# Cross-attention keys kept whole and rotated ahead, one norm's statistics used for two, all values made in the scan

## The reference

```python
xm = _ln(_ln(x, ln1_g, ln1_b), ln_g, ln_b)
xc = silu(conv3(xm @ w1_w + w1_b));  v = silu(xm @ v1_w + v1_b)
y  = _selective_ssm(xc, ...)                 # 128 channels x 16 states, scan over 256 steps
x1 = (y * v) @ w2_w + w2_b + x
a  = gelu(_ln(x1, ln2_g, ln2_b) @ ff1_w + ff1_b) @ ff2_w + ff2_b + x1
x  = _layernorm(x + a)                                          # "post0"
lat = _ln(x, ln_lat_g, ln_lat_b)                                # a norm of a norm
ctx = _ln(context, ln_ctx_g, ln_ctx_b)                          # 2 x 512 tokens
q = lat @ Wq;  k, v = split(ctx @ Wkv)                          # 16 heads of 64
k = apply_rope(k, cos, sin)
attn = softmax(clip(q k^T / 8, -11, 11))                        # per head, 256 x 512
x = _layernorm(x + (attn v) @ Wo + bo)                          # "post1"
```

## Time and profile before

| | us |
|---|---|
| three runs, median (lowest to highest) | 533.27 (531.43 to 534.46) |
| the profiled execution, whole | 532.46 |
| its span in the trace | 530.7 |
| TensorE busy | 439.2 (83%) |
| VectorE busy | 313.8 (59%) |
| ScalarE busy | 205.0 (39%) |
| POOL busy | 141.0 (27%) |

### The profile page before, as it was taken

The page is one execution under the profiler, slowest core; times in us unless marked ns, Lnnn a source line. Parts: engine busy times, 40 slices in busy tenths (PEclk is TensorE's granted clock), DMA queues, the critical chain, the costliest instruction groups (busy, mean ns, idle before and its releaser), DMA issues.

```text
span 530.7 us, 7338 instructions
## 1 busy us (share of the span) xinstructions
PE 439.2 (83%) x2780; PEld 265.4 (50%) x2788; DVE 313.8 (59%) x741; ACT 205.0 (39%) x257; POOL 141.0 (27%) x133
## 2 busy tenths in 40 slices
PE   0538978699999999889999888698567989978794
PEld 0206655354444445665777655345323544564384
DVE  4669954636766665542511487864696775236554
ACT  0555613143333233115333358774133444626500
POOL 3205643337767666400200400000100000003300
PEclk9867997989999999989999896999997999989898
DMA  8501000000004111060142230000000000010000
GB/s 305 214 25 44 2 1 0 1 2 1 0 1 158 41 41 40 19 228 1 60 64 31 49 61 0 3 3 1 0 3 0 2 2 3 1 31 0 0 1 20
DMA packets 7359, 19.37 MB, mean 37 GB/s; under 512 B 1750, under 2 KB 3126, under 8 KB 6806
## 3 DMA queue, kind: packets, MB, share of 16 engines
q1 hardware_dynamic: 7324, 18.91, 12.0%
HBM read 17.26 MB, written 1.15 MB: 35 GB/s over the span
## 4 chain that ended last, share of the span: by engine, by line
PE 40%; DVE 26%; POOL 15%; issue 13%; ACT 5%; DMA 1%; POOLq 0%; another core or an unknown queue 0%; DVEq 0%
PE ps L1190 38%; POOL big L540 7%; DVE ps L1043 4%; POOL big L547 4%; POOL rstd L490 2%; DVE ps L861 2%; DVE big L866 2%; DVE stats L773 2%; DVE mx_a L1047 2%; POOL big L522 2%; DVE normed L783 1%; ACT big L700 1%; PE ps L1202 1%; PE ps L1564 1%; DVE meanvar L776 1%
## 5 line engine op out<-in xcount | busy, mean ns | idle before, releaser
L1190 PE MATMUL ps<-big,late 128*32 128x256 f32 (+4 forms) x792 | 102.7, 386 | 12.4 <-DVE mx_x L1043 5.2
L1190 PE MATMUL ps<-late,big 128*128 128x128 f32 (+1 forms) x448 | 64.4, 276 | 3.6 <-DVE mx_x L1043 2.0
L1190 PEld LDWEIGHTS ps<-big,late 128*32 128x32 f32 (+3 forms) x800 | 39.5, 117 | 54.4 <-issue 23.1
L726 ACT ACTIVATE big<-ps 128x1024 f32<-128x1024 f32 x48 | 49.0, 1023 | 39.8 <-PE ps L1190 39.4
L488 POOL TENSOR_SCALAR vareps<-meanvar 128x4 f32<-128x4 f32 (+1 forms) x11 | 2.5, 229 | 221.1 <-DVE meanvar L776 221.1
L1190 PEld LDWEIGHTS ps<-late,big 128*128 128x128 f32 (+1 forms) x448 | 44.8, 152 | 27.4 <-issue 20.2
L664 ACT ACTIVATE big<-ps 128x1024 f32<-128x1024 f32 x32 | 32.8, 1024 | 64.8 <-PE ps L1190 47.0
L540 POOL TENSOR_TENSOR big<-big 128x512 f32<-128x512 f32 x32 | 40.5, 1267 | 43.2 <-DVE big L926 43.2
L1043 DVE CUSTOM_DVE_ANT_0 ps<-ps,big 128x512 f32<-128x512 f32 x64 | 42.5, 718 | 12.1 <-PE ps L1190 9.1
L1190 PE MATMUL ps<-big 64*128 64x256 f32 (+1 forms) x320 | 47.5, 410 | 1.7 <-POOL big L547 1.0
L926 DVE TENSOR_SCALAR big<-big 128x1024 f32<-128x1024 f32 x32 | 25.3, 790 | 39.7 <-ACT big L664 39.7
(11 more groups left out here) (231 smaller groups left out, 686.0 us busy)
## 6 DMA issues: line engine op xcount, KB each, us to landing
attn_w<-in_w_x SPq DMA_DIRECT2D x1, 2560.0 KB, 13.2
big<-parts_kx SPq DMA_DIRECT2D x18, 128.0 KB
late<-in_w_up SPq DMA_DIRECT2D x1, 2048.0 KB, 7.7
late<-in_w_dn SPq DMA_DIRECT2D x4, 512.0 KB, 4.0
attn_w<-in_w_up SPq DMA_DIRECT2D x1, 1024.0 KB, 6.4
attn_w<-in_w_dn SPq DMA_DIRECT2D x1, 1024.0 KB, 9.3
parts_kx<-ctx_r SPq DMA_DIRECT2D x1, 768.0 KB, 4.4
rowv<-in_rowv SPq DMA_DIRECT2D x1, 576.0 KB, 3.8
```

What stands on the lines that cost most here:

```text
L726: nc.scalar.activation(ex1[:, n % 3, :].rearrange("p (r n) -> p r n", r=2), ps[:, 2 * (n % 2):2 * (n % 2) + 2, :], ACT.Exp, scale=scale).t ...
L1190: return nc.tensor.matmul(o, lhsT, rhs, start=start, stop=stop, skip_group_check=shared)
```

## The change

1. **Room for all keys.** `kT0` becomes eight tiles, two where they were and six in the region `mid`, which is free after the scan. The buffers of the products move to `dtmp` and one piece of `big1`.
2. **Keys ahead.** Nine tiles (`K_FIRST`) are made ahead of the loop, in banks that a table names. In the loop one tile for each pair follows (9 to 15, pairs 0 to 6): the query at u = 0, key halves at u = 1 and 2, nothing at u = 3. All `idle_work` between the scan and the loop goes.
3. **Values.** All 16 groups are made in the scan, one a step from step 0.
4. **One norm for two.** The statistics of `summed` serve post0 and lat: with variance v the second norm of a normed row has the factor (v(1 + eps) + eps^2)^-0.5. POOL computes this root first and post0's behind it; VectorE writes `normed` (lat) first, then rotates tiles 6 to 8, then writes `x`.
5. **POOL's order.** After ln2's root and after the two roots, POOL waits until the normalised tiles are written, before it goes on with rotations and residual sums.
6. **ScalarE's tables.** A dummy activation with Gelu before ln2's transposes and with Exp after the Gelus loads the function tables there. The sign product of `rope0` moves ahead of the scan.

```diff
-NORMS = ("ln1", "ln", "ctx", "ln2", "post0", "lat", "post1", "post2", "post3", "post4", "post5")
+NORMS = ("ln1", "ln", "ctx", "ln2", "lat", "post0", "post1", "post2", "post3", "post4", "post5")
-        kT0 = big1(0, [P, 2, B * CS])
+        kT0 = [big1(1024 * c, [P, B * CS]) if c < 2 else mid(5120 - 1024 * (c - 2), [P, B * CS])
+               for c in range(NPAIR)]
+        kt1 = (dtmp[:, 0, :], dtmp[:, 2, :])
+        kt2 = (dtmp[:, 1, :], big1(3584, [P, CS]))
+        FF_BANKS = (0, 3, 5)
+        K_FIRST = 9
+        def key_banks(n):
+            return ((6, 7), (6, 7), (4, 3), (1, 2), (6, 7), (4, 3), (6, 7), (5, 2))[n] if n < 8 else (7, 6)
```

On POOL:

```diff
+            rotated0(0)
             root("ln2")
+            pool.wait_ge(norm_out, normed_tiles("ln2"))
+            for n in (1, 2, 3):
+                rotated0(n)
             pool.wait_ge(S["x2_done"], 1)
             link(nc.gpsimd.tensor_tensor(resid[:], x[:], rv4("ff2_b"), ALU.add))
             nc.gpsimd.tensor_tensor(resid[:], resid[:], x2[:], ALU.add).then_inc(S["res_ready"], 1)
-            for b in range(B):
-                rotated0(0, b)
-            root("post0")
-            root("lat")
-            rotated0(1, 0)
+            rotated0(4)
+            k = NORMS.index("lat")
+            pool.wait_ge(norm_var, k + 2)
+            link(nc.gpsimd.tensor_scalar(vareps[:, 0:NJ], meanvar[:, k, 0:NJ, 1], 1.0 + EPS, EPS * EPS,
+                                         ALU.mult, ALU.add))
+            nc.gpsimd.tensor_tensor(rstd[:, k, 0:NJ], vareps[:, 0:NJ], neghalf[:, 0:NJ],
+                                    ALU.pow).then_inc(norm_rstd, 1)
...
+            nc.gpsimd.tensor_tensor(rstd[:, k + 1, 0:NJ], vareps[:, 0:NJ], neghalf[:, 0:NJ],
+                                    ALU.pow).then_inc(norm_rstd, 1)
+            pool.wait_ge(norm_out, normed_tiles("lat"))
+            for n in range(5, K_FIRST):
+                rotated0(n)
             pool.wait_ge(norm_out, normed_tiles("post0"))
             nc.gpsimd.tensor_tensor(resid[:], x[:], rv4("bo0"), ALU.add).then_inc(S["res_ready"], 1)
...
-                if u in (0, 3) and 2 <= c + 1 < NPAIR or n == 3:
-                    rotated0(c + 1, u // 3)
+                if u == 2 and K_FIRST + c < B * NPAIR:
+                    rotated0(K_FIRST + c)
```

On ScalarE:

```diff
-                u = s - 3
-                if 0 <= u < V_EARLY:
-                    evac0(u // 2, f"v{u % 2}")
+                if s:
+                    evac0((s - 1) // 2, f"v{(s - 1) % 2}")
...
+            set_table(ACT.Gelu)
             to_cols(xT[:], 0, "xT_ps", "xT_done", v("ln2_g"), v("ln2_b"), 2)
...
+            set_table(ACT.Exp)
             to_cols(xT[:], 0, "xT_ps", "xT_done", v("lat_g"), v("lat_b"), 3)
```

On VectorE:

```diff
+            rotary(0)
             dve.wait_ge(S["y_ps"], NG // 4)
...
-            layernorm("ln2", x2[:], normed)
+            layernorm("ln2", x2[:], normed, lambda: rotary(1))
+            for n in (2, 3, 4):
+                rotary(n)
...
-            add_and_norm(4, "ff2_ps", 1, 2, "post0")
+            link(nc.vector.tensor_tensor(flat(summed), ps[:, 1, :], flat(resid), ALU.add))
...
+            rotary(5)
+            for i, dst in enumerate((normed, x)):
+                dve.wait_ge(norm_rstd, k + i + 1)
+                for j in range(NJ):
+                    nc.vector.tensor_scalar(dst[:, j, :], summed[:, j, :], meanvar[:, k, j, 0:1],
+                                            rstd[:, k + i, j:j + 1], ALU.subtract, ALU.mult
+                                            ).then_inc(norm_out, 1)
+                if i == 0:
+                    for n in range(6, K_FIRST):
+                        rotary(n)
-            layernorm("lat", x[:], normed, lambda: rotary(1, 0))
...
+                    if u == 2 and K_FIRST + c < B * NPAIR:
+                        rotary(K_FIRST + c)
```

On TensorE, in the scan and in the loop:

```diff
-                if 0 <= s - 2 < V_EARLY:
-                    values0((s - 2) // 2, s % 2)
+                values0(s // 2, s % 2)
...
-                if 2 <= c + 1 < NPAIR or c == 0 and u:
-                    project0(c + 1, u)
+                later = K_FIRST + c
+                if c + 1 < NPAIR and u == 0:
+                    pe.wait_ge(S["k0_mul"], 2 * later)
+                    mm(ps[:, 6, :], w_x0[:, c + 1, 3, :], xT[:]).then_inc(S["q0_ps"], 1)
+                elif c + 1 < NPAIR and u == 1:
+                    keys0(later, (0,))
+                elif c + 1 < NPAIR and u == 2:
+                    pe.wait_ge(S["q0_done"], c + 2)
+                    keys0(later, (1,))
```

139 lines of the change are left out of this document (68 added, 71 removed).

## The result

| device us | before | changed |
|---|---|---|
| median (four runs each, same chip) | 532.57 | 506.54 |
| lowest to highest | 531.43 to 534.46 | 506.17 to 507.45 |
| ratio, 95% interval | 1 | 0.951 (0.948 to 0.954) |
| profiled execution: time, span | 532.46, 530.7 | 506.76, 505.0 |

The change takes 26.0 us off; 22.5 were forecast. The direction was right and so were most of the steps; the size was not. Two executions of the kernel before, of 655 and 735 us at mean clocks of 0.65 and 0.57, are left out of every comparison.

What follows compares the result with a forecast made beforehand. TensorE ends nearly every chain, VectorE bounds the scan, and no engine is full from 70 to 111 us. 10.0 up to the first mix plus 12.5 in the loop, 22.5 us less, gave 510.8 us, range 507.5 to 518.0.

Steps and rivals of the forecast that it cites:

- The scan: Scan, 40 to 70 us: all 16 value groups in its steps cost 0.1 us, from 0 to 1.2.
- End of scan to ff2: Up to the residual sum behind ff2: 5.1 us sooner, of it norm 2.0, clock 2.0, one key half less 0.9.
- rival (b): Norms before the loop: TensorE's clock isn't kept through their pauses; 515 us, chance 0.14.
- ff2 to the loop: From the residual sum to the loop's first logits: these start at 96.9 instead of 107.08 us, -10.2 in all.
- the root: POOL's second root beside the latents' normalisation: costs 0.3 us, between 0 and 0.8 if it blocks VectorE.
- The first pass: Loop start: first mix 4.5 us behind the logits (3.2 to 5.8), at 101.4 against 111.44, -10.0.
- The loop: Cross-attention loop: fewer TensorE fillers make a head pair 12.35 us instead of 14.25, in all -12.5.
- rival (a): Loop doesn't shrink fully: a clip waits behind a reciprocal or POOL, TensorE waits at the fourth place; 518 us, chance 0.13.
- Rival (c): Before the loop: keys ahead lie on the path, so work only moves; 10.3 us come back, 521, chance 0.05.
- Rival (d): Better than forecast: no meeting with POOL at all, -2 us, 508, chance 0.08.
- The step that failed: Last pair, tail and everything from 227 us on: as before, no change in time.

Runs made afterwards that it cites:

- the second trace of the kernel before: The kernel before, run again with no edit, in the single execution whose trace is read: 534.49 us.
- the copy: The changed kernel, run again with no edit: 509.27 us, ratio 0.955.
- two copies: The changed kernel, run again twice with no edit: 509.27 us and, in a single execution, 505.9 us.

## Why the prediction was right or wrong

**The scan: it costs nothing, and the 0.1 is luck.** I took 0.1, between 0 and 1.2. VectorE's second and third products start at 42.13 and 43.98, the step of 1.85, and norm ln2 at 78.70, 0.1 later than before. But the first spread of the scan already starts 0.1 later (38.47 for 38.36), so the scan added 0. The lone run of the values gave no difference.

**End of scan to ff2, right.** -5.1 forecast, -4.7 measured (92.42 to 87.74). The norm gives its 2.05 and the ff matmuls 1.93, each at its forecast 2.0; against the second trace of the kernel before the ff matmuls give 2.65, so the close agreement of that term is in part luck. The runs with the waits alone and without the waits point to the keys as what keeps the clock, as the step had it; the shorter pause, which I named against rival (b), isn't enough (4.51). Rival (b) did not come: clock 1.00 from 82 on.

**ff2 to the loop, right; the root mis-sized.** 96.93 against 96.9, from a residual sum 0.4 later: the stretch itself was 9.2 and not 9.55. I took 0.3 for the second root beside the normalisation, between 0 and 0.8; two traces say 0 (1.12 and 1.11). By the rule of the Trainium skill that the prediction names ("SBUF — State Buffer", section "Who interferes with whom") it would have been 0.8. The traces agree with it in that each POOL operation of 128x512 seen here costs the norm about 1.0 (2.06, 2.09, 2.16 for 1.11); for an operation on 128x4 it does not show.

**The first pass, mis-sized by 1.1.** The step put the mix 4.5 behind the logits; it came 3.43 behind. The sum began with key tile 8's two products behind the logits' start. In fact the first of them waits only for the tile's first half and starts at 96.18, 0.75 before the logits, which is 0.6 of the error. The x tiles took 2.06 where I had 2.4, which is most of the rest. That they, and not the clip, would meet POOL was right, here; the runs show that the order is what decides it.

**The loop, right.** A pair takes 12.35, as worked out, and putting the fillers back returns 12.1 of the 12.5. The 0.4 that is missing lies in the first pair. There a clip beside a POOL operation takes 1.56, and the mix behind it comes 0.27 later than in the pairs that follow; the next one, behind a clip of 1.21, comes 0.12 later (112.67). That is what rival (a) had, but in the first pair and not in every one:

```profile
107.80 1.56 DVE L966 TENSOR_SCALAR big<-big 128x1024 f32<-128x1024 f32 x1 [0.38 <-ACT big L688]
...
109.42 1.08 PE L1228 MATMUL ps<-big,late 128*64 128x256 f32 x8 [0.21 <-DVE big L966]
```

Rival (c), keys ahead as mere displacement, fell with this: both gains stand at post1's root. Rival (d) named the right side with the wrong reason; the meeting with POOL took place.

**The step that failed** is one sentence: "The last pair, the tail and everything from 227 us on are as before". As a mean that may hold. But it was taken as a fixed number from one trace, and the same code takes 296.2 to 301.1 us in the twelve traces that have it. Of the 4.3 us between 510.8 and 506.54, 0.7 is the edited part up to post1's root (-22.5 forecast, -23.2 measured: the first pass 1.1 better, the loop 0.4 worse), and 2.5 is that spread. The last 1.0 is a term of the same kind: I added 0.8 because the median of the three runs lay so far above the profiled execution, and in the result the changed kernel's median lies 0.2 below its own. The result's four runs drew the short side of the spread (506.2 to 507.5), the copy's mostly the long one (506.35 to 509.94). The range had bounds for every edited term and none for this. With 2.5 us more below its low end of 507.5 it would have begun at 505.0. What makes the untouched part vary is shown in part only: half clock at different matmuls behind post1, and an open remainder later on.

**What is additive.** The waits alone give 5.3 and the one norm alone 5.8 at post1's root, the fillers 12.1 from the first mix to there, together 23.2, which is what the whole change gives. This agreement is luck: undone in the whole, the waits are worth 1.0 before the loop and not 5.3, and the kernel before differs from its own copy by 0.85 at that root. The keys ahead have no lone run; in the whole they cover part of what the waits cover alone, most likely since they keep the clock.

## What to carry to other kernels

Where a vector operation on the path starts at the same signal as a queue of big POOL operations, let POOL wait for it: on the kernel before, two such waits brought the loop forward by 5.3 us, 4.0 by the operations themselves and most of the rest by the clock of the query behind the second. Look for what else fills the gap before adding up such gains, and count with a later POOL operation meeting the next vector operation instead. Choose a milestone on the engine that the next stage waits for: at post1's root most of a loss of 1.0 us seemed regained, and at TensorE's transposes 5 us later the loss was still there. A range needs a term for the part that is not edited: take two traces of the same kernel, subtract them stage by stage, and use what they differ by.

## What the runs showed of the hardware

- A VectorE tensor-scalar of four 128x128 tiles takes 1.11 alone, 1.11 to 1.12 beside a POOL operation of 128x4 (1.04 to 1.13 long), 2.06 to 2.16 beside one of 128x512, and 3.07 to 3.17 beside two.
- It works in the other direction too: POOL's 128x512 sum at 99.79, begun beside a clip, took 1.65 instead of 1.27.
- Three matmuls of 512 columns behind a norm took 4.51 to 5.46 where TensorE had idle work and a pause of 0.9 or more before the transposes, and 2.81 where key matmuls stood there, with pauses of 0.49 and 1.53.
- The mean granted clock of one and the same stage was 0.91 in one execution and 0.98 in another, with 2.7 us between them. The Trainium skill ("TensorE: Matmul & The Clock Gate", section "Part 1: The HAM clock gate (the "warmup" mystery)") calls the warm-up run-variable and puts the penalty of the ramp under 1% of a typical kernel's span. The traces agree that it varies: the same four matmuls behind the same pause took 2.07, 1.87 and 1.26. The page's figure is for a ramp, and here the clock falls and rises many times and is not the whole difference, so no run tests it; two copies differ by 3.7 us, or 0.7%.
